# One scatter wait in the expert stages, setup loads in another order, and copied rows for the last groups, in a one-core transformer kernel

## The reference

```python
x = x + attn_a(_layernorm(x))   # layernorm, 16 heads with a relative-position bias and softmax, projection, then a 128-512-128 MLP
x = x + ffn(_layernorm(x))      # mixture of 8 experts
x = x + attn_b(_layernorm(x))   # gated linear recurrence over time, layernorm
x = x + ffn(_layernorm(x))      # the same mixture of experts again
```

## Time and profile before

| | us |
|---|---|
| median of 3 runs | 1586.89 |
| lowest, highest | 1567.63, 1593.62 |
| the profiled execution | 1580.79 |
| its span | 1579.1 |

### The profile page before, as it was taken

How to read it: one execution, slowest core, us unless ns; L and a number is a source line. 1 busy time by engine, 2 the same in 40 slices (tenths; PEclk the granted TensorE clock), 3 DMA queues, 4 the chain that set the end, 5 groups by cost and what they waited for, 6 DMA issues and landing times. The chain is left out here.

```text
span 1579.1 us, 37919 instructions
## 1 busy us (share of the span) xinstructions
PE 1221.4 (77%) x11689; PEld 1026.9 (65%) x11689; DVE 1147.3 (73%) x3844; ACT 939.0 (59%) x2010; POOL 999.7 (63%) x1149
## 2 busy tenths in 40 slices
PE   3789999999999999972888878577777368888760
PEld 1557777777777777751888778456555257887750
DVE  5289999999999999855556555488888546555538
ACT  2388888888888888741444444366666235444420
POOL 5245688888888888765455555248788735555530
PEclk9599999999999999985889998598899578899965
DMA  7111111111111111142222222112222122222228
GB/s 212 54 54 45 45 58 58 58 60 58 58 58 59 58 60 58 39 120 59 76 75 76 76 73 69 54 55 74 76 82 61 54 72 76 75 74 81 69 72 278
DMA packets 98674, 117.18 MB, mean 74 GB/s; under 512 B 17784, under 2 KB 78768, under 8 KB 98480
## 3 DMA queue, kind: packets, MB, share of 16 engines
q1 hardware_dynamic: 69904, 74.23, 16.4%
q0 software_dynamic: 16896, 35.16, 6.5%
q10 hardware_dynamic: 11680, 5.39, 1.3%
HBM read 47.56 MB, written 41.51 MB: 56 GB/s over the span
## 5 line engine op out<-in xcount | busy, mean ns | idle before, releaser
L1119 DVE TENSOR_TENSOR ebuf<-score_banks,region 128x768 f32<-128x768 f32 x256 | 243.6, 951 | 20.3 <-PE score_banks L830 15.5
L1362 ACT ACTIVATE region<-ebuf 128x768 f32<-128x768 f32 x256 | 215.9, 860 | 24.1 <-DVE ebuf L1119 23.2
L1340 ACT CAST copied<-max_banks 128x768 bf16<-128x768 f32 x256 | 205.8, 804 | 25.6 <-PE max_banks L818 23.4
L1776 POOL DMA_INDIRECT choice_rows<-second_yo,second_xg x136 | 131.3, 965 | 130.2 <-DVE second_yo L1896 99.9
L1776 POOL DMA_INDIRECT choice_rows<-first_yo,first_xg x136 | 131.4, 966 | 129.7 <-DVE first_yo L1896 98.7
L1646 POOL DMA_INDIRECT expert_rows<-d_rows,a_d_index x128 | 145.8, 1139 | 32.5 <-issue 21.2
L2195 POOL DMA_INDIRECT expert_rows<-d_rows,z_d_index x128 | 130.4, 1018 | 38.6 <-issue 32.0
L1852 ACT ACTIVATE second_silu<-second_bgu,second_biases 128x256 f32<-128x256 f32 (+1 forms) x144 | 62.7, 465 | 128.2 <-PE second_bgu L1805 58.3
L1852 ACT ACTIVATE first_silu<-first_bgu,first_biases 128x256 f32<-128x256 f32 (+1 forms) x144 | 62.8, 464 | 128.0 <-issue 57.2
L1888 DVE SCALAR_TENSOR_TENSOR first_hT<-first_bgu,first_biases,first_silu 128x256 f32<-128x256 f32 (+1 forms) x144 | 63.3, 464 | 74.8 <-ACT first_silu L1852 44.0
L1888 DVE SCALAR_TENSOR_TENSOR second_hT<-second_bgu,second_biases,second_silu 128x256 f32<-128x256 f32 (+1 forms) x144 | 63.3, 464 | 73.1 <-ACT second_silu L1852 45.6
(11 more groups left out here) (349 smaller groups left out, 4408.2 us busy)
## 6 DMA issues: line engine op xcount, KB each, us to landing
region_r<-region_r SPq DMA_DIRECT2D x192, 128.0 KB
first_xg<-expert_rows SPq DMA_DIRECT2D x64, 132.0 KB
second_xg<-expert_rows SPq DMA_DIRECT2D x64, 132.0 KB
z_rows<-choice_rows SPq DMA_DIRECT2D x32, 256.0 KB
c_rows<-choice_rows SPq DMA_DIRECT2D x16, 512.0 KB
out<-xres ACTq DMA_DIRECT2D x16, 256.0 KB
choice_rows<-first_yo,first_xg POOLq DMA_INDIRECT x136
choice_rows<-second_yo,second_xg POOLq DMA_INDIRECT x136
```

The source lines that it names most:

```text
L1119: nc.vector.tensor_tensor(ebuf[:, half_of_ebuf(c, j), :, :], score_banks[:, :, 0:BK], bias32[:, plain(j), :], ALU.add).then_inc(scores_fre ...
L1340: nc.scalar.copy(copied[:, 2 * j:2 * j + 2, :], max_banks[:, :, 0:BK]).then_inc(maxed_free, 1)
L1362: nc.scalar.activation(p32[:, j % 4, :, :], ebuf[:, half_of_ebuf(c, j), :, :], ACT.Exp).then_inc(exped, 1)
L1776: pool.indirect_dma_start(choice_dram, bass.IndirectOffsetOnAxis(ap=xg[:, i % G, t, E:E + 1].bitcast(I32), axis=0), yo[:, i % 4, t, :], No ...
```

## The change

In the expert stages, POOL waits before the scatters of turn i also until the down product of turn i + 1 is done (for the last turn, its own). In setup, ACT's queue first loads the weight rows and then the first part of x; the small vectors go to SP's queue between the steps of the position table; `hank` is loaded in four parts and each bias block waits for its own; the first bias blocks come after the weight transposes; two thirds of the operand fills go from DVE to ACT; x is loaded in four parts of 8, 16, 20 and 20 tiles, each with its own semaphore for which the first normalisation that needs it waits, the last of them issued after setup; the padding rows are stored in the third attention body. At the end of both routing stages, the rows of the last two groups (m = 14, 15) are copied by DVE into a ring place that is free, with the second label, and all eight scatters of a group follow each other without the wait for landing and without the relabelling; the last row_apply on POOL moves before them. The padding rows behind the experts are written as soon as the experts' ends are known, half of them from ACT's queue in both stages, and half of the weight split moves into the last bodies.

```diff
+    def late(self, m):
+        return m >= self.s.B // 2 - 2
+
+    def spare(self, m):
+        return (2 * m - self.s.DEPTH // 2) % self.s.DEPTH
+
+    def copy_rows(self, m):
+        ring, spare, E = 2 * m % self.s.DEPTH, self.spare(m), self.s.E
+        self.nc.vector.tensor_copy(self.rows[:, spare:spare + 2, :, 0:E], self.rows[:, ring:ring + 2, :, 0:E])
+        return self.nc.vector.tensor_copy(self.labels(spare), self.w["dest"][:, 1, 4 * m:4 * m + 4])
...
-    def find(self, ch):
+    def find(self, ch, known):
         s, w, V, NE = self.s, self.w, self.nc.vector, self.s.NE
         used, starts, changes, J = self.used, w["starts"], w["changes"], 2 * NE + 1
-        ch.mark(V.tensor_copy(w["pad_at"][:], w["base"][:]))
+        V.tensor_copy(w["pad_at"][:], w["base"][:]).then_inc(known, 1)
...
+    X_PARTS = (0, 8, 24, 44, s.TILES)
+
+    def load_x(engine, q):
+        at = slice(X_PARTS[q], X_PARTS[q + 1])
+        engine.dma_start(xres[:, at, :], x_dram[:, at, :]).then_inc(x_in[q], 16)
...
+        HC = H // 4
+
+        def hankel(q):
+            return bass.AP(tensor=scratch.tensor, offset=q * HC * 3 * P, ap=[[1, P], [3 * P, HC], [1, 2 * P]])
...
+                def vector(dst, src):
+                    sp.dma_start(dst, src).then_inc(loaded, 16)
 
                 sp.wait_ge(padded, 1)
                 sp.dma_start(relpad[:, P - 1:P - 1 + s.S], ins["L0_attn_a_rel_pos"][:, 0:s.S]).then_inc(rel_in, 16)
+                vector(gcol[:, 0:1], col("L0_attn_a_ln1_g"))
+                vector(gcol[:, 1:2], col("L0_attn_a_ln1_b"))
+                vector(gcol[:, 2:3], col("L0_attn_a_ln2_g"))
                 sp.wait_ge(rel_in, 16)
                 sp.dma_start(scratch, relpad[:]).then_inc(rel_out, 16)
+                vector(gcol[:, 3:4], col("L0_attn_a_ln2_b"))
+                vector(inbcol[:, 2:3], ins["L0_attn_a_in_proj_b"][2 * s.E:3 * s.E].rearrange("(p a) -> p a", a=1))
+                vector(outb[:], row("L0_attn_a_out_b"))
+                vector(b2[:], row("L0_attn_a_b2"))
                 sp.wait_ge(rel_out, 16)
-                sp.dma_start(hank[:], hankel).then_inc(rel_tab, 16)
-                sp.wait_ge(loaded, 16 * (NLOADS + 1))
                 for q in range(4):
-                    n = s.TILES // 4
-                    sp.dma_start(xres[:, q * n:(q + 1) * n, :], x_dram[:, q * n:(q + 1) * n, :]).then_inc(x_in, 16)
-                sp.wait_ge(pads_made, 1)
-                for rows_dram, at in ((pads_dram, 0), (slots_dram[s.SPARE:s.SPARE + s.NE * P, :], s.NE)):
-                    sp.dma_start(rows_dram.rearrange("(n p) c -> p n c", p=P), pad_rows_sb[:, at:at + s.NE, :]).then_inc(pads_left, 16)
-                sp.wait_ge(x_in, 64)
-                sp.wait_ge(rel_tab, 16)
+                    sp.dma_start(hank[:, q * HC:(q + 1) * HC, :], hankel(q)).then_inc(rel_tab[q], 16)
+                load_x(sp, 1)
+                load_x(sp, 2)
+                for q in range(4):
+                    sp.wait_ge(rel_tab[q], 16)
...
-                    (gcol[:, 0:1], col("L0_attn_a_ln1_g")), (gcol[:, 1:2], col("L0_attn_a_ln1_b")),
-                    (gcol[:, 2:3], col("L0_attn_a_ln2_g")), (gcol[:, 3:4], col("L0_attn_a_ln2_b")),
-                    (inbcol[:, 2:3], ins["L0_attn_a_in_proj_b"][2 * s.E:3 * s.E].rearrange("(p a) -> p a", a=1)),
                     (rrow[:], ins["L0_ffn_router_w"]),
-                    (outb[:], row("L0_attn_a_out_b")),
-                    (b2[:], row("L0_attn_a_b2")),
-                ] + [(b1ld[:, c:c + 1], ins["L0_attn_a_b1"][c * P:(c + 1) * P].rearrange("(p a) -> p a", a=1))
-                     for c in range(FF // P)]
-                for dst, src in loads:
-                    act.dma_start(dst, src).then_inc(loaded, 16)
+                ):
+                    act.dma_start(dst, src).then_inc(rows_in, 16)
+                act.dma_start(b1ld[:], ins["L0_attn_a_b1"].rearrange("(c p) -> p c", p=P), allow_slow_non_contiguous=True).then_inc(loaded, 16)
                 for c in range(2):
                     act.dma_start(inbcol[:, c:c + 1], spread_col(c), allow_slow_non_contiguous=True).then_inc(loaded, 16)
-                assert len(loads) + 2 == NLOADS + 1
+                load_x(act, 0)
+                act.wait_ge(ones_made, 1)
+                many = ones[:].rearrange("p (a q) -> p a q", a=1).broadcast_to([P, 8, P])
+                for n in range(1, RING):
+                    nc.scalar.activation(qs[n].rearrange("p j (b q) -> p (j b) q", b=2), many, ACT.Copy, scale=0.0)
+                    nc.scalar.copy(ks[n].rearrange("p j (b q) -> p (j b) q", b=2), many).then_inc(cleared, 1)
...
-                for n in range(RING):
-                    for j in range(4):
-                        nc.vector.tensor_scalar(qs[n][:, j, 0:P], ones[:], 0.0, None, ALU.mult)
-                        nc.vector.tensor_scalar(qs[n][:, j, P:2 * P], ones[:], 0.0, None, ALU.mult)
-                        nc.vector.tensor_copy(ks[n][:, j, 0:P], ones[:])
-                        nc.vector.tensor_copy(ks[n][:, j, P:2 * P], ones[:])
-                take_bias(0)
-                take_bias(1)
-                dve.wait_ge(loaded, 16 * (NLOADS + 1))
...
-                take_bias(2)
-                take_bias(3)
-
+                take_bias(0)
+                take_bias(1)
+                dve.wait_ge(loaded, VECTORS)
...
+                    pe.wait_ge(rel_tab[2 * j // HC], 16)
...
-                pe.wait_ge(rel_tab, 16)
-                turn_bias(0)
-                turn_bias(1)
-                pe.wait_ge(loaded, 16 * (NLOADS + 1))
+                pe.wait_ge(rows_in, ROWS_IN)
...
+                if 2 * c in X_PARTS:
+                    dve.wait_ge(x_in[X_PARTS.index(2 * c)], 16)
...
+                if d.late(m):
+                    for k in range(2):
+                        dve.wait_ge(scattered[k][m % 2], 64 * (m // 2))
+                    d.copy_rows(m).then_inc(d_copied, 1)
...
+                if b == B + 2:
+                    later.split(dve, ch, range(s.NE // 2))
+            tables.find(ch, known).then_inc(found, 1)
...
-            later.split(dve, ch)
+            later.split(dve, ch, range(s.NE // 2, s.NE))
...
+            act.wait_ge(known, 1)
+            pad_rows(act, s, w, slots_dram, pads_dram, range(s.NE // 2), padded)
...
+            load_x(sp, 3)
             for b in BODIES:
                 body(b)
+                if b == -2:
+                    sp.wait_ge(pads_made, 1)
+                    for rows_dram, at in ((pads_dram, 0), (slots_dram[s.SPARE:s.SPARE + s.NE * P, :], s.NE)):
+                        sp.dma_start(rows_dram.rearrange("(n p) c -> p n c", p=P), pad_rows_sb[:, at:at + s.NE, :]).then_inc(pads_left, 16)
...
+            sp.wait_ge(known, 1)
+            pad_rows(sp, s, w, slots_dram, pads_dram, range(s.NE // 2, s.NE), padded)
             sp.wait_ge(tabled, 1)
-            pad_rows(sp, s, w, slots_dram, pads_dram, range(s.NE), padded)
...
+            def scatter_late(c):
+                m = group(c)
+                if m is None or not d.late(m):
+                    return
+                pool.wait_ge(d_placed, m + 1)
+                for k, first in enumerate((2 * m % DEPTH, d.spare(m))):
+                    if k == 1:
+                        pool.wait_ge(d_copied, m - (B // 2 - 2) + 1)
+                    for t in range(4):
+                        pool.indirect_dma_start(
+                            slots_dram, bass.IndirectOffsetOnAxis(ap=d.index[:, m % 2, k, t:t + 1], axis=0),
+                            d.rows[:, first + t // 2, t % 2, :], None).then_inc(scattered[k][m % 2], 16)
+
             def body(b):
                 relabel(b - 7)
                 scatter(b - 6, 0, 0)
                 scatter(b - 7, 1, 0)
                 normed(b - 1, (b - 1) % RING)
-                row_apply(b - 4)
+                if b - 4 < B - 1:
+                    row_apply(b - 4)
...
+                if b - 3 == B - 1:
+                    row_apply(b - 3)
+                scatter_late(b - 5)
...
                 for i in range(ST):
+                    pool.wait_ge(y_full, min(i + 2, ST))
                     pool.wait_ge(y_done, i + 1)
...
+                    elif d.late(m):
+                        pool.wait_ge(d_copied, m - (B // 2 - 2) + 1)
+                        first = d.spare(m)
...
+                        if d.late(placed_in(i)):
+                            scatter(placed_in(i), 1)
...
+                act.wait_ge(known, 1)
+                pad_rows(act, s, w, slots_dram, pads_dram, range(NE // 2), padded)
                 act.wait_ge(d_sorted, 1)
                 nc.scalar.activation(exps, exps, ACT.Exp).then_inc(d_exped, 1)
                 act.wait_ge(tabled, 1)
-                pad_rows(act, s, w, slots_dram, pads_dram, range(NE // 2), padded)
```

More of the change, by code:

```diff
@@ L564, in _ @@
                 nc.vector.tensor_copy(w["router"][:], pw[3][:, s.E:s.E + s.NE])
-                take_bias(6)
-                take_bias(7)
```

(21 more changed lines are left out.)

43 lines of the change are left out of this document (27 added, 16 removed).

## The result

The changed kernel took 1530.18 us (median of 6 runs, 1516.78 to 1533.98) against 1584.6 (6 runs) for the kernel before; the ratio is 0.965, interval 0.9617 to 0.9682. The profiled execution took 1527.64 with a span of 1525.9, 53.2 us under the 1579.1 of before. Of these, 8.2 lie ahead of the first expert stage's first load (745.42 to 737.24; setup gave 6.6), 22.5 and 24.5 in the two expert stages (first load to last scatter), 0.3 in combine; the recurrence took 2.4 more.

The account below looks back on a forecast made before the run. PE and POOL both wait 1 us a turn because runs of scatters delay PE's results. 1580.8 - 10 - 4 - 3.4 - 46.6 + 2 = 1518.8, times 1.0039: 1525 us; range 1465 to 1580.

Parts of the forecast that it names:

- The wait: Expert stages: POOL's new wait shortens runs of scatters, 3.17 us a turn instead of 3.54, gain 46.6 us.
- every second turn pass unheld: Expert stages: the hold catches one turn at 3.52 us, the next runs at POOL's own 2.53; 6.05 per two turns.
- a charge for silu: Expert stages: a third of the restart of ACT's silu after each hold, 0.28 us per pair, 0.14 per turn.
- Idle near 82 us: Expert stages: sign that POOL's idle time before scatters falls to near 82 us instead of 130.
- The tail: End of each expert stage: the last but one turn waits for the last down product; +2 us taken.
- Setup: Before attention: earlier transposes, split `hank` and no wait for x; -10 us, bounds 0 and -14.
- End of attention: Last 16 scatters without landing waits, split's half in DVE's 6.84 us idle time; -4 us, bounds 0 and -5.
- 0.13 per copy: Copied rows: each of 4 DVE copies lengthens a scatter beside it by 0.13 us, 0.5 in all.
- End of the recurrence: Last 16 scatters there without waits for landing; -3.4 us, bounds 0 and -4.
- Free flow: Expert stages: one hold-off lets PE's results pass, 2.55 to 2.95 us a turn, 1446 to 1497 us; chance 0.15.
- no gain: Expert stages: the hold catches every turn, 3.5 us as now, only the rest counts, 1571 us; chance 0.28.
- Slower: Expert stages: serial chain of 6.4 us in some turns; one in four gives 3.91 a turn, 2% slower; chance 0.08.

Follow-up runs that it names:

- experiment 1: The kernel before with only POOL's new wait added in the two expert stages; 1546.87 us against 1589.81, ratio 0.9736.
- experiments 11 and 12: The changed kernel with the whole split of the expert weights back after the tables; 1521.39 us in one run, then timed at 1537.39 us, ratio 0.9672.
- experiment 4: The changed kernel with finished rows stored to fixed places by plain stores on SP's queue instead of POOL's indirect scatters; 1429.49 us in one run.
- experiment 5: The kernel with plain stores on SP's queue, but POOL waits as in the changed kernel and fills a scratch tile per former scatter; 1440.37 us in one run.

## Why the prediction was right, point by point

**The sum.** Taken were -46.6 + 2 for the wait, -10, -4 and -3.4, in all -62.0 us; the traces show -47.0, -6.6, -1.6, +2.4 and -0.3 in combine. The wait carries the result, and the other three terms were all put too high.

**The wait.** The pitch was put at 3.17 and came at 3.161 and 3.167, which is 47.2 us less for the two stages. The size fits better than the reasons, and that is in part luck: I had every second turn pass unheld (3.52 and 2.53) with a charge for silu. In the trace most turns are alike, 2.23 us of run and 0.91 to 0.94 of pause, and silu and `yo` start 0.82 and 0.97 us after a run of two, not 1.1 to 1.24 as after the run of four. The hold was put too long and too seldom, and the two errors cancelled.

The wait was expected to do its good by shorter runs alone. The experiments show two effects. It ends the runs of six, in which PE itself stands still (3.69 us a turn before). And it lets POOL start on a `yo` that has long been written: before, a run starts 0.28 us after the end of DVE's `yo`, now mostly 0.27 after PE's signal, in the row of 854.37 even ahead of the next `yo`. Estimated from the table, the 42 turns in runs of four before give 42 x (3.39 - 3.14) = 10.5 us of the first stage's gain and the 21 turns in runs of six 21 x (3.69 - 3.14) = 11.6. A run of two was not needed: a limit of four with `yo` ready costs nearly the same. The prediction has no term for the granted clock, though PE's busy time per turn fell with it.

Of the signs, each stage came at 233 to 235 us for 230. "Idle near 82 us" was a slip: it takes the gain of both stages from one. 130 less 23.3 is 107, and 107.4 and 105.8 came.

**The tail.** +2 was taken. From turn 63's scatter to the last one's end it was 21.6 and 24.6 us before, 23.7 and 20.5 after; over the traces of the variants it lies between 15.9 and 26.2, so this term can't be read.

**Setup.** -10 was taken, -6.6 came. Transposes and a split `hank` worked; the failed step is the end, which I put near 24. It is set by the chain of biases, PE to DVE to ACT, and DVE's scaling of weights now stands in its middle, 4.49 us of idle ACT. The size varies: in the traces with this setup attention starts between 27.1 and 30.8, in the two with the old one at 33.9 and 34.2.

**End of attention.** -4 was taken, -1.6 came (first load after attention's start: 711.2 to 709.6; experiment 1, with the old code there, had 709.1, so one trace can't settle so small a term). The last 16 scatters took 21.8 us where I had 20.2. POOL waited 1.47 us for DVE in front of the moved `row_apply`, and the split that I had costed at nothing in DVE's idle time cost POOL 0.8 + 0.4 + 0.5 us. The cover was right for DVE and forgotten for POOL.

On the price of DVE copies beside a scatter: the row of before said 1.09. The scatter of 1.32 us has 0.67 us of such copies beside it and is 0.36 longer, so my 0.13 per copy was too low. The one of 1.49 has none: the copy ahead of it ended at 713.70 and it starts at 713.78, beside DVE's subtraction of 0.69 us. The three scatters of 1.48 us in this trace and those of experiments 11 and 12 also start just as such a subtraction does. The Trainium skill, page "SBUF — State Buffer", section "SBUF: two separate sides", says that a copy by DVE of this kind locks POOL out of writing descriptors while it runs. The traces agree in direction, with 0.36 us for 0.67 of copies; the 1.49 is not explained by it.

**End of the recurrence.** -3.4 was taken, +2.4 came. The 16 scatters did take 3.2 us less, but the step "the padding rows start earlier and are not last", made for attention's end and carried over, failed: they are last. SP's four stores took 15.60 us beside scatters without a pause, 8.12 before. That explains why nothing was won, 27.5 us against 27.3 from the first of the 16 scatters to the load. The other 2.2 us lie ahead of those scatters; that stretch took 244.8 us, 242.6 before, and 241.8 to 248.4 over the traces of the variants, so they are not shown to be the change's doing.

**Free flow** is refuted for this form of wait and **no gain** as well. The rule of the Trainium skill, page "SBUF — State Buffer", section "SBUF: two separate sides", that PE and ACT are never shut out of their memory, on which I rested part of "no gain", isn't contradicted: PE multiplies inside a run. What is late are the signals, and of those the rule says nothing; experiment 4 removes the lateness with the scatters. **Slower** did not happen with this wait but did with one every third turn, at 3.86 to 3.98, about the 3.91 I had as the point for 2% (one such turn in four would give 3.98, so the two did not quite match). The starved chain is like the one described, its place the run of six.

**What stays open.** The traces show when signals pass, not what blocks them; that scatters and signals share a path is inferred. Plain stores issued by POOL, or scattered rows without POOL, would tell the making of a scatter from its writes; neither was run. Whether a scatter of 256 rows at once would shorten the hold was not tried either.

## What to carry to other kernels

Where a queue of software-made indirect transfers runs beside a pipeline on signals, look at what happens in the run of transfers and just after it, not at busy shares: a wait that bounds the runs and lets the queue start only when its data have long been ready can be worth more than starting early. Removing a pause from such a run may only move the time to whoever used the pause; ask who that is. And a step moved under one engine's idle time must be checked against the other engine that it slows.

## What the hardware showed unexpectedly

- A run of scatters holds back many of PE's signals that fall due in it, not all; the first one behind it comes later the longer the run: 0.64 us after two, 1.02 after four, 1.40 after six.
- Unbroken scatters also stretch SP's own stores: four take 12.2 to 15.6 us instead of 8.1. Where such stores run beside them, DVE's chain of small steps takes 17.6 us instead of 6.8; with the stores later it takes 8.2.
- POOL's fills beside DVE (experiment 5) made DVE's copies of 128x512 take 1.04 us instead of 0.42 and those of 128x4 0.86 instead of 0.16, while its operations on two inputs stayed at 0.41 and 0.47.
